# Layer 1 of a two-layer megakernel: a second timetable for the routing steps, double-buffered masks, a signal for each piece, and expert weights in 1 MB pieces

## The reference, cut to what matters

```python
xn = _layernorm(x, axis=-1)
x = x + attn(xn, Wq_down, Wk_down, Wv_down, ..., Wc) + ffn(xn, wg, we)

# attn: 16 heads of 8; latent projections, RoPE on half of each head
q = concat([q_c, rope(q_e)]); k = concat([k_c, rope(k_e)])
scores = where(causal, q @ k.T / sqrt(8), -inf)
y = softmax(scores) @ v;  return y.reshape(b, t, c) @ Wc

# ffn: 128 experts, each with room for C = 32 first and second choices
logits = xt @ wg;  gates = softmax(logits)
e1 = argmax(gates);  e2 = argmax(logits without e1)
loc1 = cumsum(mask1)[token, e1] - 1        # a token's place in its expert's buffer
loc2 = cumsum(mask2)[token, e2] + counts1[e2] - 1
buf[idx1] += xt * (loc1 < C);  buf[idx2] += xt * (loc2 < C)
yb = einsum('ecd,edf->ecf', buf, we)       # we: 128 x 128 x 128 float32, 8 MB
y = g1 * v1 * yb[idx1] + g2 * v2 * yb[idx2]
```

## Time and profile before

| | us |
|---|---|
| median of 3 runs | 2266.21 (2262.88 to 2268.63) |
| the profiled execution, its own time | 2265.14 |
| its span in the trace | 2263.3 |
| PE, DVE, ACT, POOL busy over the span | 1996.5, 1732.8, 1335.6, 1288.6 |
| TensorE's clock, mean granted share of full speed | 0.942 |
| layer 0 | up to about 1485 |
| layer 1, routing alone | 1498 to 1553 |
| layer 1, attention with routing | 1583 to about 2031 |
| layer 1, attention with experts, and the end | about 2031 to 2263 |

### The profile page before, as it was taken

How to read it: one execution, slowest core, us unless ns; L and a number is a source line. 1 busy time by engine, 2 the same in 40 slices (tenths; PEclk the granted TensorE clock), 3 DMA queues, 4 the chain that set the end, 5 groups by cost and what they waited for, 6 DMA issues and landing times. The chain is left out here.

```text
span 2263.3 us, 40460 instructions
## 1 busy us (share of the span) xinstructions
PE 1996.5 (88%) x13648; PEld 1155.7 (51%) x13714; DVE 1732.8 (77%) x2781; ACT 1335.6 (59%) x2421; POOL 1288.6 (57%) x972
## 2 busy tenths in 40 slices
PE   1799999999999999999999999945899999998885
PEld 0455555555555555555555555533455555544442
DVE  3498888888888889888888888854777777765544
ACT  1576776776776776766767767611355555544442
POOL 0477867767767767767768777623322222224540
PEclk9999999999999999999999999955899999998987
DMA  7514505415325335335145055041222222233437
GB/s 192 136 41 107 130 27 127 112 39 128 97 51 132 86 67 132 76 77 132 53 99 131 30 118 122 15 123 63 83 92 87 88 88 88 88 112 102 141 94 227
DMA packets 197004, 222.49 MB, mean 98 GB/s; under 512 B 28872, under 2 KB 139504, under 8 KB 192688
## 3 DMA queue, kind: packets, MB, share of 16 engines
q1 hardware_dynamic: 194736, 215.52, 37.0%
q0 software_dynamic: 2048, 4.18, 0.7%
HBM read 165.41 MB, written 54.27 MB: 97 GB/s over the span
## 5 line engine op out<-in xcount | busy, mean ns | idle before, releaser
L685 POOL TENSOR_TENSOR dBx<-REP,BC 128x1024 f32<-128x1024 f32 x256 | 603.0, 2358 | 288.2 <-DVE dA L845 243.2
L845 DVE TENSOR_TENSOR_SCAN dA<-dA,dBx 128x512 f32<-128x512 f32 x512 | 626.6, 1224 | 115.1 <-ACT dA L555 66.2
L374 PE MATMUL UP<-xnT,W 128*128 128x512 f32 x1024 | 518.4, 626 | 52.0 <-ACT hT L564 40.1
L383 PEld LDWEIGHTS DN<-W,hT 128*128 128x128 f32 x4096 | 469.4, 192 | 109.3 <-issue 97.6
L383 PE MATMUL DN<-W,hT 128*128 128x128 f32 x4096 | 496.0, 278 | 0.3 <-ACT GD L571 0.3
L564 ACT ACTIVATE hT<-UP,b 128x512 f32<-128x512 f32 x512 | 355.1, 694 | 88.7 <-PE UP L374 85.0
L555 ACT ACTIVATE dA<-REP,A 128x512 f32<-128x512 f32 x512 | 354.1, 695 | 72.4 <-DVE PR L854 72.1
L854 DVE TENSOR_TENSOR PR<-dA,BC 128x512 f32<-128x512 f32 x512 | 353.6, 691 | 31.5 <-DVE dA L845 18.8
L1705 DVE TENSOR_REDUCE NM<-S 128x4 f32<-128x1024 f32 (+1 forms) x192 | 234.5, 1221 | 148.5 <-PE S L1264 93.5
L374 PEld LDWEIGHTS UP<-xnT,W 128*128 128x128 f32 x1024 | 180.6, 195 | 278.5 <-issue 146.2
L1466 ACT ACTIVATE PT<-S 128x1024 f32<-128x1024 f32 x192 | 196.4, 1023 | 181.5 <-PE S L1278 135.2
(11 more groups left out here) (246 smaller groups left out, 2809.6 us busy)
## 6 DMA issues: line engine op xcount, KB each, us to landing
REP<-s_delta SPq DMA_DIRECT2D x128, 256.0 KB, 7.8
REP<-s_dx SPq DMA_DIRECT2D x128, 256.0 KB, 7.3
BC<-s_b SPq DMA_DIRECT2D x128, 256.0 KB, 8.7
s_parts<-SPL SPq DMA_DIRECT2D x32, 384.0 KB, 2.8
s_dx<-tz SPq DMA_DIRECT2D x16, 512.0 KB, 3.1
s_y<-zeros SPq DMA_DIRECT2D x32, 256.0 KB, 4.8
WE<-in_L_ffn_we SPq DMA_DIRECT2D x32, 256.0 KB, 4.5
YC<-s_y SPq DMA_DIRECT2D x16, 512.0 KB, 4.9
```

What stands on the lines that cost most here:

```text
L374: nc.tensor.matmul(UP[k % 2][:], W1[:, e % E0, f * P:(f + 1) * P], xnT[:, q, :], start=True, stop=True).then_inc(upf.sem, 1)
L383: last = nc.tensor.matmul(DN[:, j * P:(j + 1) * P], hT[:, e % 2, f, j * P:(j + 1) * P], W2[:, e, f, :], start=(f == 0), stop=(f == FB - 1))
L685: nc.gpsimd.tensor_tensor(dBx[:, s % 2], DX[:, h, j:j + 2, :], BC[:, q // 2, q % 2, :].unsqueeze(1).to_broadcast([P, 2, T0]), ALU.mult).th ...
L845: nc.vector.tensor_tensor_scan(h, h, dBx[:, k // 2 % 2, k % 2, :], 0.0, ALU.mult, ALU.add).then_inc(scan_done.sem, 1)
```

## The change

What it does, in five parts:

1. Routing gets a timetable of its own. Sequence n's routing base is `max(6 * n, 12 * (n - 7))` instead of `12 * (n - 7)`. The walk starts at -24 instead of -108. Sequences 0 to 14 are thus routed 6 steps apart; from 14 on everything stands where it stood relative to attention.
2. MK and ef have two buffers, and `route` is split into four signals (`picked`, `located`, `hot`, `added_up`). The waits for the shared PSUM banks are worked out from the timetable (`turns`, `front_free`, `counts_free`).
3. Some places in the timetables shift by one to three steps.
4. The constants that routing needs are loaded first on a semaphore of their own, the others are waited for by the first t1 and the first p1. The KS memsets go from DVE, ahead of its walk, to POOL, behind the second norm.
5. WE has three buffers, and each batch's weights are one DMA of 1 MB, issued behind that sequence's reload of QS, in each period from `MAPPED - 16` on.

```diff
-YBUF, WBUF = 4, 2
+YBUF, WBUF = 4, 3
...
-... ef = sb("ef", [P, J1, 2]); MK = sb("MK", [P, J1, 2, P], BF16)
+... ef = sb("ef", [P, 2, J1, 2]); MK = sb("MK", [P, 2, J1, 2, P], BF16)
...
-    PE_AT = dict(xnt=-22, g=-16, count=(-13, -10), map=-3, qk=-20, rot=-18, v=-3, p1=0, nmt=12, p2=17, pv=(21, 23, 27, 30), ot=(32, 34), yt=37, wc=41)
-    ACT_AT = dict(xT=-21, cs=(-10, -7), v=-1, spl=(-15, -12), nm=14, exp=18, osb=(26, 32), yT=39)
-    DVE_AT = dict(top=-15, mk=-13, loc=(-9, -6), oh=-4, add=-2, t1=-18, t2=-15, mx=1, nms=12, epi=(34, 37), x=42)
-    POOL_AT = dict(norm=-23, keep=-13, val=-4, qk=-16, r1=-13, spl=-11)
-    SP_AT = dict(xn=-11, parts=-8, load=-7, nm=14, nm_in=16)
-    MAPPED = HS1 * (NSEQ - 1) + R
+    PE_AT = dict(xnt=-23, g=-16, count=(-13, -10), map=-3, qk=-20, rot=-18, v=-3, p1=0, nmt=12, p2=17, pv=(21, 24, 26, 30), ot=(32, 34), yt=37, wc=41)
+    ACT_AT = dict(xT=-21, cs=(-12, -9), v=-1, spl=(-15, -12), nm=14, exp=18, osb=(26, 32), yT=41)
+    DVE_AT = dict(top=-15, mk=-13, loc=(-11, -8), oh=-7, add=-2, t1=-18, t2=-15, mx=1, nms=12, epi=(34, 37), x=42)
+    POOL_AT = dict(norm=-23, keep=-14, val=-6, qk=-15, r1=-13, spl=-11)
+    SP_AT = dict(xn=-13, parts=-8, load=-7, nm=12, nm_in=16, we=-16)
+    MAPPED = HS1 * (NSEQ - 1 - AHEAD)
...
-        for now in range(R - 24, HS1 * (NSEQ + 3)):
+        for now in range(-24, HS1 * (NSEQ + 3)):
...
+            def ahead(at):
+                for n in range(NSEQ):
+                    if routing(n) + at == now:
+                        yield n, n % BUF
...
+    def routing(n):
+        return max(HS1 // 2 * n, HS1 * (n - AHEAD))
+    def turns(*stages):
+        order = sorted((at(n), i, name, n) for i, (name, at) in enumerate(stages) for n in range(NSEQ))
+        return {b[2:]: a[2:] for a, b in zip(order, order[1:])}
...
+    FRONT = turns(("nmt", beside("nmt")), ("xnt", routed("xnt")), ("qk", beside("qk")), ("rot", beside("rot")), ("g", routed("g")), ("v", beside("v")))
+    COUNTS = turns(("count0", routed("count", 0)), ("count1", routed("count", 1)), ("map", routed("map")))
...
-            sp.dma_start(WE[:, b % WBUF, 4 * k:4 * k + 4, :], ...[:, 16 * b + 4 * k:16 * b + 4 * k + 4, :])
+            sp.dma_start(WE[:, b % WBUF], dram["L1_ffn_we"].rearrange("e d f -> d e f")[:, 16 * b:16 * b + 16, :])
...
-                    if now == MAPPED - 16 + 8 * b + 2 * k:
-                        weights(b, k)
+                if now == MAPPED + SP_AT["we"] + HS1 * b:
+                    weights(b)
...
+            if before == "g":
+                pe.wait_ge(top.sem, top.at(k, 4))
...
+            if before == "map":
+                pe.wait_ge(added_up.sem, added_up.at(k, 1))
+            elif before:
+                pe.wait_ge(located.sem, located.at(k, 2 if before == "count0" else 4))
+                pe.wait_ge(carried.sem, carried.at(k, 1 if before == "count0" else 2))
...
+            if now == POOL_AT["norm"] + HS1 // 2:
+                for i in range(BUF):
+                    last = nc.gpsimd.memset(KS[i][:], 1.0)
+                last.then_inc(poolset, 1)
...
-        for i in range(BUF):
-            last = nc.vector.memset(KS[i][:], 1.0)
...
-                dve.wait_ge(route.sem, route.at(n - 1, 8))
+                dve.wait_ge(mapped.sem, mapped.at(n - 2, 1))
...
-                if now == FINAL[g] + 6:
+                if now == FINAL[g] + 8:
```

More of the change, by code:

```diff
@@ L1181, in load, with half @@
                     sp.dma_start(out, part).then_inc(parts_in.sem, 16)
-        def half(due, now):
-            for n, m in due(R + SP_AT["xn"]):
+        def half(due, ahead, now):
+            for n, m in ahead(SP_AT["xn"]):
                 sp.wait_ge(kept.sem, kept.at(n, 1))
@@ L1205, in half @@
                 load(0, QS, n, m)
+            for b in range(BATCHES):
+                if now == MAPPED + SP_AT["we"] + HS1 * b:
+                    weights(b)
             for n, m in due(SP_AT["nm"]):
@@ L1224, in half @@
                         sp.dma_start(YC[:, g % 2, c, :, :], yv[:, c, 8 * g:8 * g + 8, :]).then_inc(y_loaded[g % 2], 16)
-                if g < 7 and now == FINAL[g] + 9:
+                if g < 7 and now == FINAL[g] + 11:
                     sp.wait_ge(added, g + 1)
@@ L1338, in half @@
             for n, m in due(PE_AT["rot"]):
-                pe.wait_ge(rope.sem, rope.at(n, 1))
+                front_free("rot", n)
                 for q, w in enumerate((wqr, wkr)):
@@ L1432, in _, with half @@
         nc.scalar.activation(stats[:, :, 0], q1[:], ACT.Sqrt).then_inc(root_done, 1)
-        def half(due, now):
-            for n, m in due(R + ACT_AT["xT"]):
+        def half(due, ahead, now):
+            for n, m in ahead(ACT_AT["xT"]):
                 act.wait_ge(fr_x.sem, fr_x.at(n, 1))
@@ L1444, in half @@
             for j in range(J1):
-                for n, m in due(R + ACT_AT["cs"][j]):
+                for n, m in ahead(ACT_AT["cs"][j]):
                     act.wait_ge(counted.sem, counted.at(n, j + 1))
@@ L1502, in _, with half @@
         pool.wait_ge(stat_step, 12)
-        def half(due, now):
-            for n, m in due(R + POOL_AT["norm"]):
+        def half(due, ahead, now):
+            for n, m in ahead(POOL_AT["norm"]):
                 def wide(v):
@@ L1559, in _ @@
     def _(dve):
-        for s in (top, rope, route, max_done, nm_step, epi, x_upd):
+        for s in (top, rope, picked, located, hot, added_up, max_done, nm_step, epi, x_upd):
             dve.sem_inc(s.sem, LEAD * s.per)
@@ L1631, in half @@
                 nc.vector.tensor_tensor(t2[:], fr, wide(sin), ALU.mult).then_inc(rope.sem, 1)
-            for n, m in due(R + DVE_AT["top"]):
+            for n, m in ahead(DVE_AT["top"]):
                 dve.wait_ge(fr_g.sem, fr_g.at(n, 1))
```

151 lines of the change are left out of this document (80 added, 71 removed).

## The result

The changed kernel takes 2255.6 us (median of 5 runs, 2249.22 to 2259.05); the kernel before 2266.21 in the same set (5 runs). The ratio is 0.9943, with a 95% interval of 0.9926 to 0.9961: 10.6 us faster, where 30 were forecast. The profiled execution took 2259.05 us, with a span of 2257.3. On another chip the changed kernel had 0.9934 (0.991 to 0.9959).

What follows compares the result with a forecast made beforehand. TensorE was taken to bound attention with one routing sequence per period. Head -53, doubled periods +35 and expert stretch -12 sum to -30 on 2265.1 us: 2235, forecast as 2236 us, range 2211 to 2260.

Steps and rivals of the forecast that it cites:

- Part 1, the head: Start of layer 1: seven routing sequences ahead of the first Q and K go, first scores 53 us sooner.
- Part 2, the doubled periods: Attention periods 0 to 6, two routing sequences in each: 23.7 us per period, 5.0 more, 35 us in all.
- The second limit: Periods with two routing sequences: SP's reload of QS keeps each from being under 21.5 us.
- Part 3, the steady periods: Periods 7 to 21: shifted steps go into idle time of DVE and ACT; nothing, 3 us to either side.
- Part 4, the expert stretch: Periods beside the experts: weights issued behind the reload of QS gain 12 us, a third of 36 over steady.
- rival C: Expert stretch: the 1 MB piece delays the maxima's and parts' store, gaining nothing or losing up to 9; 2253 us, chance 0.17.
- Part 5, the end: After the last attention sequence: FINAL's adds two steps later change nothing.
- D: Periods with two routing sequences: FR bank stalls and half clock give back all of the head; 2278 us, chance 0.10.
- B: Periods with two routing sequences cost only what SP's reload forces, about 2.8 us each, 20 in all; 2221 us, chance 0.20.

Runs made afterwards that it cites:

- experiment 4: Changed kernel with two PV steps put back, and map moved from step -3 to -6 and add from -2 to -4: ratio 0.9815 to the kernel before.
- experiment 1: Changed kernel with two of the four PV steps put back where they were before (23 and 27): 2255.66 us, ratio 0.9885 to the kernel before.
- experiment 2: Changed kernel with four buffers of QS and KS instead of three, PV as changed: ratio 0.9918 to the kernel before.
- experiment 9: Changed kernel with the weights of only the first three expert batches loaded: 226.1 us from sequence 22 to 31.
- experiment 8: Changed kernel with PV back, map early, four WE buffers and the 1 MB piece ahead of the reload: ratio 0.985 to the kernel before.
- experiment 13: Kernel before without any expert batch (weights, gathers, expert matmuls and scatters left out): 175.7 us from sequence 22 to 31.
- experiment 11: Changed kernel without any expert batch (weights, gathers, expert matmuls and scatters left out): 182.5 us from sequence 22 to 31.
- experiment 3: Kernel before with only the new weight loading (three WE buffers, one 1 MB piece per period behind the reload): ratio 0.998 to the kernel before.

## Why the prediction was wrong, point by point

**Part 1, the head: right.** -53 us forecast, -53.0 and -52.6 measured from the first XN. From the first wq to the first scores (1534.77) it took 33.6 us, 33 forecast, 29.5 before. The wq stood at 1501.2, not 1496, because POOL's XN came at 1499.3 where it had come at 1494.0; in the second pair it came 3.6 us earlier than before's instead, so this is the spread of layer 0, not the change. POOL's KS memsets take 5.29 us for three, 1.76 each as on DVE, within the 0 to 2 us that I allowed. They end at 1506.6, and POOL's sum of t1 and t2 starts at 1507.17, released by DVE: covered, as costed.

**Part 2, the doubled periods: right, and 4 us too dear by a count.** They take (1677.3 - 1559.2) / 5 = 23.6 us in the mean against 23.7 forecast, 5.1 over before's 18.5; the waits are those named, map about 0.9 and g about 0.5. The clock was not 1.00 throughout, as forecast: the first of the five began at half clock and took 25.3 us, the next three, at full clock, 23.5 each. But there are six such periods, not seven: from sequence 6 to 7 both kernels take 18.5 to 18.8 us. Moving map earlier takes 2.9 us off each (experiment 4 against 1). That the first row maximum of sequence 7 stands at 1696.03 us, where I forecast 1696, is luck: the first scores came 5 us late, with layer 0, and one doubled period fewer made up for it. The second limit that I gave, a reload that can't end under 21.5 us, was not seen: at 21.5 us in the mean (experiment 4, single periods 21.0) TensorE waits for row maxima and xnT, not for QS. What lies lower wasn't tested.

**Part 3, the steady periods: the step that failed.** I wrote "Same work; the places of pv, count, loc and cs shift a step or two, into idle time of DVE and ACT. Nothing". I looked at where the shifted steps went on the engines that do them, and not at who waits for what stands behind them on TensorE. In Part 2 I had even found that SP's reload leaves "no slack", and listed what SP had queued ahead of it; its wait for the second pass of n - 3 I did not follow back. With two PVs of 0.8 us ahead of the last unit of that pass, the release came late, the reload 0.96 us later after the first scores than before (5.90 for 4.94 us, means of sequences 8 to 21), and 15 such periods are the 13.9 us of the measured difference. Reload to scores stayed at 13.8 us. Two of the fifteen periods, from 13 and from 18, took 20.95 us: there TensorE waited 1.7 and 1.6 us for the reload, and its clock was at half for 3.4 us, from 1813.9 and from 1912.9. The kernel before has full clock in the whole stretch. Experiments 1 and 2 show the cause from both sides.

**Part 4, the expert stretch: the gain was a third of a wrong remainder, and what was gained there was given back.** The direction of the first half holds: with no WE issue ahead of it, the parts' store goes out 0.8 us earlier in the period (3.5 to 2.7 us; 0.6 in the second pair). The 2 us that I read from the earlier trace rows are those of one period. With the WE issue gone, SP is held by the next in its queue, the maxima's store: in sequences 27 to 29 of the changed kernel the parts' store still goes out 2.7 to 3.9 us after POOL's last split, right behind the maxima's store, where it was 3.8 to 5.2. Then the reload waits again for the second pass of n - 3 (+0.2), and its landing takes longer (15.0 to 15.8 us to the scores; 15.3 to 15.6 in the second pair), at least partly because 1 MB now runs behind it (experiment 9). Ahead of the reload it costs 1.0 us more than the old pieces (experiment 8). The landings of the weights and of the store, from the DMA views of the expert stretch of before and after (KB, median us from issue to landing):

```profile
WE<-in_L_ffn_we SPq DMA_DIRECT2D x32, 256.0 KB, 4.5
s_parts<-SPL SPq DMA_DIRECT2D x9, 384.0 KB, 3.6
```

```profile
s_parts<-SPL SPq DMA_DIRECT2D x9, 384.0 KB, 2.8
...
WE<-in_L_ffn_we SPq DMA_DIRECT2D x8, 0.5 KB, 10.7
```

(The last row is the 1 MB pieces; the size that the view gives for them, 0.5 KB, is not that of the transfer.)

The store itself lands sooner than before, 2.8 us instead of 3.6. So rival C's place is wrong too. The store is issued some 10 us after the 1 MB (2107.78 and 2097.50 in one period), and the 1 MB lands 10.7 us after its issue, so little of it can still be ahead. The Trainium skill (DMA: Bandwidth & Descriptors, Queues, rings and completion order) says that each DMA engine takes the descriptors of a ring in order. That order alone gives no reason why the reload, which is ahead of the 1 MB, should suffer; the 14.0 and 14.3 against 15.9 us show that it does. What carries that, no run told.

And the size was wrong from the start. I set the stretch's cost at 36 us over steady, "of which at least 1 us is expert work". Experiments 13 and 11 put it so: without any experts the stretch still takes 175.7 us (before) or 182.5 (after), 6.9 us and 13.7 us over nine steady periods of 18.76. So some 7 of the 36 us are there without any expert. Of the rest, 14 us are the gathers on the chip where that was measured. Weights, matmuls and scatters share what remains, and no run separates the last two.

**Part 5, the end: nothing forecast, 5 to 7 us gained.** Without experts the kernel before has 59.7 us there (experiment 13) and the changed one 56.0 (experiment 11), so most of the gain is not in the experts' work; part 5 alone has 63.7 (experiment 3). Of parts 1 to 3 and FINAL's later adds I tested none singly for it, so this stays open.

**The rivals.** C gave 2253 us and came nearest to 2255.6, but by a mechanism that isn't there. That is luck, and so is it that the time lies within the stated range: the sum allowed 3 us either way for the steady periods, and they took 14. D's stall of the FR bank did not come, g waits 0.6 us at most, nor did its half clock: that is there only in the first 12 us of these periods. The doubled periods did not fall to B's 20 us in all, though the best version came near: 21.5 us each is 2.8 over steady, B's own price, by taking map's wait away.

**A version that beats both.** PV back and map early, in either way of loading weights: ratios 0.9815, 0.9835, 0.985, 0.981 and 0.9822 on three chips, 38 to 47 us under the kernel before, where the change alone has 0.994. With four buffers of QS and KS on top it has 0.9832 on a fourth chip.

## What to carry to other kernels

When a step is moved, follow its engine's queue onwards from it: list which waits of other engines are released by something that now stands behind it, buffer releases above all, and look whether the waiter has slack. A loop of reload, scores and release sets a period of its own, and it shows in no engine's busy share; take it out of the trace by its three legs before giving a gain to any one of them. And before taking a stretch's excess for the cost of what runs there, run it with that left out.

## What the runs showed that I had not expected

Without routing and without experts a period of attention is not shorter than with routing: 19.5 us beside 18.8, although TensorE has 17.2 us of work in it (155.0 / 9) against 18.1 (343.4 of 356 us, 19 periods). TensorE then waits for the reload in eight of nine periods; why the loop is longer than beside routing is not shown.

The chips differ by 0.7% on the kernel before (2266 to 2283 us). In the changed kernel's traces the difference lies in one place: its stretch from sequence 22 to 31 takes 203 and 206 us on two chips, 217 on a third, and on that one 203 without gathers. So the difference goes with POOL's indirect gathers. That it is they that run slower there was not measured by itself.
